# One add in four of the softmax sums is made by an accumulating DMA that GpSimd issues, in place of GpSimd's own add

## The chip, the core and the metric

One core of one Trainium2 chip. The metric is the time of one execution of the program on the device in microseconds (us), the median of several. TensorE is called PE in the profile, VectorE DVE, ScalarE ACT, GpSimd POOL and SyncE SP.

## What is computed

A small language model tower over 4096 tokens (2 sequences of 2048), width 1024, all in fp32. The attention is what the change touches: 32 heads of 32, 8 key and value heads, causal. Cut to that:

```python
h = tok_ref(x)                                # sum of 4 table rows per token, plus a bias
qkv = layernorm(h) @ w_qkv.T + b_qkv          # q: 32 heads, k and v: 8 heads, rope on q and k
scores = einsum('bhqd,bhkd->bhqk', q, k) / sqrt(HEAD_DIM)
scores = where(causal, scores, -1e20)
attn = softmax(scores, axis=-1)
out = einsum('bhqk,bhkd->bhqd', attn, v)
h = h + out @ w_o.T + b_o
h = h + ffn_ref(layernorm(h))                 # one matrix plus a low-rank Fourier update
```

## The kernel before, in words

The program has three parts. `part_a` gathers the token tables into the tile `hbuf` with indirect DMAs from GpSimd (L291): for each tile of 128 tokens one plain gather and three that add, 512 KB each, each waiting for the one before it on the same tile. In the first two chunks two tiles alternate, later four. It then makes q, k and v. `part_c` makes the output product and the last layer. Between them `part_b` does the attention, and only there does the change reach.

`part_b` goes over 16 groups of 4 heads (4 query heads share a key head). In a group, `score_steps` lists 36 steps (c, i): 256 queries c against 256 keys i, with i = c, the diagonal, first. A step has two halves of 128 keys. For each half PE makes the scores into PSUM (`st_ps`, L1097), on the diagonal VectorE adds the mask (L1012), and ScalarE takes the exponential into `probs` (L932), a ring of 8 steps in SBUF of 128 x 1024 fp32 per half. Meanwhile PE and VectorE prepare the row maxima of later rows (L1058, L984, L982), in three PSUM banks (`mx_ps`). Three steps (`LAG`) behind the scores PE multiplies `probs` with the values (L1113, `values`).

The denominators of the softmax are row sums of `probs`. To spare PE three quarters of them, GpSimd adds the tiles of `probs` first: `sum_sets` pairs the steps, and `set_sum` adds the four halves of a pair into one of four tiles `sums` of 128 x 1024 fp32, with three adds: L899 (first half plus second), L901 (plus the third), L907 (plus the fourth). PE then multiplies `sums` once with a column of ones (L1130, `denominators`), right behind the values of the pair's last step, and waits there for the sum. Of the 20 sets of a group 12 are pairs of two plain steps, 4 are pairs with a diagonal step (their last add is half as wide, 128 x 512), and 4 are a diagonal step alone (one add of 128 x 512, L895). In the last group five sets, three plain ones among them, are not summed (`unsummed`): PE takes their tiles itself (L1141).

Each engine runs its own queue in order. GpSimd's waits: for the exponential that an add reads (`exp_waited`), for its own last add (`Steps.do` waits for the semaphore that it raised), and for PE to be done with the `sums` tile that it writes again four sets later. ScalarE waits before it overwrites a slot of `probs` for the batch of values and for the sum that read it, eight steps earlier. SyncE issues the loads of the next group's queries (L89), keys (L95) and values as the present group is done with their tiles, and stores results.

Of the kernel before, what the change touches and what calls it, by code (L numbers as in the profile page):

```python
# [17 lines left out]
P = 128  # L18
# [5 lines left out]
ALU = mybir.AluOpType  # L24
# [28 lines left out]
GROUPS = ALL_HEADS // GROUP  # L53
# [497 lines left out]
STEPS, MAXES = score_steps(), max_units()  # L551
# [7 lines left out]
SLOTS, SUM_SLOTS = 8, 4  # L559
# [16 lines left out]
SETS = sum_sets()  # L576
SET_OF = [j for j, steps in enumerate(SETS) for s in steps]
# [3 lines left out]
def unsummed(g, j):  # L581

    return g == GROUPS - 1 and j in DIRECT


def sums_made(g, j):

    return g * len(SETS) + sum(not unsummed(g, k) for k in range(j + 1))


LEAD, FIRST_LEAD = 17, 14
DIAGONAL_ROOM = 0.55
TURN_AFTER = 5
# [48 lines left out]
def part_b(nc, hand, w0_hi, w0_lo, q_hi, q_lo, k_hi, k_lo, v_dram, o_dram, den_dram, recip_dram, w_o_t, w_base_t,  # L642
           w1_dram, enc, fourier_t):

    with ExitStack() as ctx:
        sb = lambda n, s, d: ctx.enter_context(nc.sbuf_tensor(n, s, d))
        sem = lambda n: ctx.enter_context(nc.semaphore(n))
# [40 lines left out]
        m_hi_done, m_rows = sem("m_hi_done"), sem("m_rows")  # L688
        st_ready, st_masked, exp_done = sem("st_ready"), sem("st_masked"), sem("exp_done")
        sum_step, sum_done, batch_done = sem("sum_step"), sem("sum_done"), sem("batch_done")  # L690
        od_copied = sem("od_copied")
        LOAD, STORE = 3 * 16, 2 * 16
        block = ctx.enter_context(nc.Block())
# [162 lines left out]
        @block.gpsimd  # L856
        def _(pool):
            nc.gpsimd.memset(k_score[M_ROW:P, :].bitcast(F32), 1.0).then_inc(k_ones_done, 1)
            pool.wait_ge(k_ones_done, 1)
            pool.wait_ge(enc_hi_done, 1)  # L860
            nc.gpsimd.tensor_tensor(enc_lo[:], enc_sb[:], enc3[0:R].bitcast(F32), ALU.subtract).then_inc(enc_lo_done, 1)
            pool.wait_ge(enc_lo_done, 1)
            pool.wait_ge(tw_hi_done, 1)
            pool.wait_ge(tw_done, 1)
            nc.gpsimd.tensor_tensor(tw_lo[:], tw[:], tw3[0:R].bitcast(F32), ALU.subtract).then_inc(tw_lo_done, 1)
            pool.wait_ge(tw_lo_done, 1)
            for c in range(DC):
                pool.wait_ge(base_in[c], 16)
                pool.wait_ge(delta_taken, c + 1)
                nc.gpsimd.tensor_tensor(hand.base[:, c, :], hand.base[:, c, :], hand.four[c][:], ALU.add  # L870
                                        ).then_inc(w1_ready, 1)

            for t in range(TPC):
                pool.wait_ge(hand.v_stored[t], 16 * CHUNKS)
            for s in range(2):
                pool.wait_ge(hand.rot_stored[s], 16 * CHUNKS * QK_TILES)
            step = Steps(pool, sum_step, 0)

            def probs_of(g, s, k, lo):
                return probs[:, (g * NS + s) % SLOTS, k, :, lo:QW]  # L880

            def exp_waited(g, s, k):
                pool.wait_ge(exp_done, 2 * (g * NS + s) + k + 1)

            def set_sum(g, j):

                q = sums_made(g, j) - 1
                at = sums[:, q % SUM_SLOTS]
                diagonal = [s for s in SETS[j] if STEPS[s][0] == STEPS[s][1]]
                wide = [(s, k) for s in SETS[j] for k in range(2) if k == 0 or s not in diagonal]  # L890
                if q >= SUM_SLOTS:
                    pool.wait_ge(batch_done, last_use[q - SUM_SLOTS] + 1)
                if len(wide) == 1:
                    exp_waited(g, diagonal[0], 1)
                    nc.gpsimd.tensor_tensor(at[:, :, P:QW], probs_of(g, diagonal[0], 0, P),  # L895
                                            probs_of(g, diagonal[0], 1, P), ALU.add).then_inc(sum_done, 1)
                    return
                exp_waited(g, *wide[1])
                step.do(nc.gpsimd.tensor_tensor(at, probs_of(g, *wide[0], 0), probs_of(g, *wide[1], 0), ALU.add))  # L899
                exp_waited(g, *wide[2])  # L900
                step.do(nc.gpsimd.tensor_tensor(at, at, probs_of(g, *wide[2], 0), ALU.add))  # L901
                if diagonal:
                    lo, last = P, (diagonal[0], 1)
                else:
                    lo, last = 0, wide[3]
                exp_waited(g, *last)
                nc.gpsimd.tensor_tensor(at[:, :, lo:QW], at[:, :, lo:QW], probs_of(g, *last, lo), ALU.add  # L907
                                        ).then_inc(sum_done, 1)

            summed = [(g, j) for g in range(GROUPS) for j in range(len(SETS)) if not unsummed(g, j)]  # L910
            last_use = [g * NS + SETS[j][-1] for g, j in summed]
            for g in range(GROUPS):
                for j in range(len(SETS)):
                    if not unsummed(g, j):
                        set_sum(g, j)

        @block.scalar
        def _(act):

            def exps(g, s, half):  # L920
                c, i = STEPS[s]
                n, lo = g * NS + s, P if i == c and half == 1 else 0
                if i == c:
                    act.wait_ge(st_masked, 2 * (g * QH + c) + half + 1)
                else:
                    act.wait_ge(st_ready, 2 * n + half + 1)
                if half == 0 and n >= SLOTS:
                    g_old, s_old = divmod(n - SLOTS, NS)
                    act.wait_ge(batch_done, n - SLOTS + 1)
                    if not unsummed(g_old, SET_OF[s_old]):  # L930
                        act.wait_ge(sum_done, sums_made(g_old, SET_OF[s_old]))
                nc.scalar.activation(probs[:, n % SLOTS, half, :, lo:QW], st_ps[:, half, :, lo:QW], ACT.Exp,  # L932
                                     scale=float(HD) ** -0.5).then_inc(exp_done, 1)

            def take(g, c):
                act.wait_ge(batch_done, g * NS + LAST_OF[c] + 1)
                if g * QH + c >= 2:
                    act.wait_ge(stored[c % 2], STORE * (g * (QH // 2) + c // 2))
                nc.scalar.copy(od_sb[:, c % 2], od_ps[:]).then_inc(od_copied, 1)  # L939

            def weight_high(c, n):
                cols = slice(n * 512, (n + 1) * 512)
                act.wait_ge(w_raw_in, 16 * (c + 1))
                nc.scalar.copy(w0_hi[:, c, cols], w_raw[:, cols]).then_inc(w0_hi_done, 1)

            def group(g, first, last):
                for s in range(NS):
                    k = s - LAG - 1
                    if k % NS in LAST_OF and not (first and k < 0):
                        take(g if k >= 0 else g - 1, LAST_OF.index(k % NS))  # L950
                    for half in range(2):
                        exps(g, s, half)
                    if 0 <= g - W_O_GROUP < DC and s in (8, 10):
                        weight_high(g - W_O_GROUP, (8, 10).index(s))

            act.wait_ge(enc_in, 16)
            nc.scalar.copy(enc3[0:R], enc_sb[:]).then_inc(enc_hi_done, 1)
            act.wait_ge(tw_ready, DC)
            nc.scalar.activation(tw3[0:R], slot_ps[0][0:R, :], ACT.Identity, scale=SCALING).then_inc(tw_hi_done, 1)
            nc.scalar.activation(tw[:], slot_ps[0][0:R, :], ACT.Identity, scale=SCALING).then_inc(tw_done, 1)  # L960
            for c in range(DC):
                act.wait_ge(delta_ready, c + 1)
                nc.scalar.copy(hand.four[c][:], slot_ps[(c + 1) % 2]).then_inc(delta_taken, 1)
            groups(group)
            take(GROUPS - 1, QH - 1)
# [78 lines left out]
        def _(pe):  # L1044
# [73 lines left out]
            def denominators(g, s):  # L1118

                c, i = STEPS[s]  # L1120
                n, j = g * NS + s, SET_OF[s]
                q = sums_made(g, j) - 1
                lo = P if SETS[j] == (s,) else 0
                pe.wait_ge(sum_done, q + 1)
                if lo:
                    for h in range(GROUP):
                        nc.tensor.matmul(od_ps[h * HD:(h + 1) * HD, 1, 0:lo], ones[:], probs[:, n % SLOTS, 0, h, 0:lo],
                                         start=False, stop=False)
                for h in range(GROUP):
                    mm = nc.tensor.matmul(od_ps[h * HD:(h + 1) * HD, 1, lo:QW], ones[:],  # L1130
                                          sums[:, q % SUM_SLOTS, h, lo:QW], start=False, stop=s in LAST_OF)
                return mm
# [412 lines left out]
```

## Time and profile before

| | us |
|---|---|
| median of 3 runs | 3373.97 (3373.56 to 3375.6) |
| the profiled execution's own time | 3371.2 |
| its span, first to last instruction | 3369.4 |
| PE busy | 3236.2 (96%) |
| GpSimd busy | 2245.7 (67%) |
| VectorE busy | 2391.3 (71%) |
| ScalarE busy | 1423.1 (42%) |
| mean granted clock of PE | 0.988 |

The profile is one execution. A row of the groups of instructions gives line, engine, operation, the tile written and those read, shapes, the number of instructions, then the busy time in us and the mean of one in ns, then the idle time just ahead of them and what ended it. A timeline row gives start and duration in us of a run of equal instructions. The attention stage runs from about 738 to 2610 us.

### The profile page before, as it was taken

How to read it: one execution, taken by the hardware profiler on the slowest of the kernel's cores; microseconds unless marked ns; L12 is line 12 of the kernel's file. 1: busy time of each engine (PE TensorE's matmuls, PEld its weight loads, DVE VectorE, ACT ScalarE, POOL GpSimd, SP SyncE). 2: the span in 40 equal slices, each digit the busy share in tenths (PEclk: the TensorE clock that was granted, in tenths of full speed). 3: DMA queues.
4: the chain of work that ended last, by engine and by line, in shares of the span. 5: the costliest groups of instructions: out<-in, count | busy, mean ns of one | idle time of the engine just before them, and what ended most of it. 6: DMA issues, size and time to landing. Idle time of an engine off the chain costs nothing. (4 is left out here: it accounts for less than half of the span.)

```text
span 3369.4 us, 59196 instructions
## 1 busy us (share of the span) xinstructions
PE 3236.2 (96%) x23824; PEld 2288.1 (68%) x23824; DVE 2391.3 (71%) x4362; ACT 1423.1 (42%) x1679; POOL 2245.7 (67%) x1033
## 2 busy tenths in 40 slices
PE   1899999999999999999999999999999899999999
PEld 1778888846666666666666666666665688888887
DVE  3667777678888888888888888888883544444443
ACT  2222222235665666666566656656656200100110
POOL 3443330049999999999999999999998222332331
PEclk8999999989999999999999999999999999999999
DMA  9999994561221222122122212212221343433342
GB/s 240 242 253 230 233 234 147 147 198 42 68 63 38 63 65 59 43 73 63 43 58 66 54 43 69 57 43 55 60 57 35 120 95 96 93 86 100 92 90 63
DMA packets 248270, 335.04 MB, mean 99 GB/s; under 512 B 64371, under 2 KB 153715, under 8 KB 247995
## 3 DMA queue, kind: packets, MB, share of 16 engines
q1 hardware_dynamic: 229562, 264.13, 29.0%
q0 software_dynamic: 18432, 67.12, 9.3%
q8 instruction: 188, 3.08, 0.4%
q14 instruction: 88, 0.71, 0.1%
HBM read 227.73 MB, written 101.71 MB: 98 GB/s over the span
## 5 line engine op out<-in xcount | busy, mean ns | idle before, releaser
L932 ACT ACTIVATE probs<-st_ps 128x1024 f32<-128x1024 f32 (+1 forms) x1152 | 1066.5, 974 | 673.4 <-PE st_ps L1097 447.2
L984 DVE TENSOR_REDUCE mpart<-mx_ps 128x1 f32<-128x512 f32 (+2 forms) x1728 | 1092.0, 683 | 196.8 <-PE mx_ps L1058 132.3
L1058 PE MATMUL mx_ps<-k_max,qs 96*128 96x512 f32 (+3 forms) x2560 | 844.2, 399 | 9.8 <-DVE mpart L984 3.2
L1097 PE MATMUL st_ps<-qs,k_score 98*128 98x512 f32 (+1 forms) x2304 | 668.3, 390 | 0.0
L1058 PEld LDWEIGHTS mx_ps<-k_max,qs 96*128 96x128 f32 x2560 | 438.8, 190 | 315.5 <-DVE mpart L984 162.3
L901 POOL TENSOR_TENSOR sums<-sums,probs 128x1024 f32<-128x1024 f32 x252 | 607.4, 2410 | 20.5 <-ACT probs L932 0.8
L899 POOL TENSOR_TENSOR sums<-probs 128x1024 f32<-128x1024 f32 x252 | 601.4, 2386 | 17.4 <-ACT probs L932 12.9
L1113 PE MATMUL od_ps<-probs,vs 128*32 128x256 f32 (+1 forms) x9216 | 589.4, 373 | 1.4 <-ACT od_sb L939 1.4
L907 POOL TENSOR_TENSOR sums<-sums,probs 128x1024 f32<-128x1024 f32 (+1 forms) x252 | 531.4, 2109 | 19.8
L1097 PEld LDWEIGHTS st_ps<-qs,k_score 98*128 98x128 f32 x2304 | 421.0, 190 | 99.2 <-ACT probs L932 24.0
L1301 POOL TENSOR_TENSOR h<-h,bb 128x1024 f32<-128x1024 f32 x32 | 104.2, 3257 | 509.5 <-DVE xn_c L1375 509.5
L1113 PEld LDWEIGHTS od_ps<-probs,vs 128*32 128x32 f32 x9216 | 240.8, 109 | 252.9 <-issue 147.4
L291 POOL DMA_INDIRECT hbuf<-in_tok_table,idx_all x128 | 194.8, 1522 | 305.9 <-DMA hbuf<-in_tok_table,idx_all 164.1
L982 DVE CUSTOM_DVE_ANT_0 mx_ps<-mx_ps,masks 128x384 f32<-128x384 f32 (+1 forms) x512 | 312.3, 645 | 53.9 <-PE mx_ps L1058 52.4
L493 PE MATMUL qk_ps<-x_hi,w_hi 128*128 128x512 f32 x640 | 253.5, 396 | 17.4 <-ACT rotation L345 15.1
L493 PE MATMUL qk_ps<-x_lo,w_hi 128*128 128x512 f32 x640 | 251.0, 392 | 0.0
L493 PE MATMUL qk_ps<-x_hi,w_lo 128*128 128x512 f32 x640 | 250.7, 392 | 0.0
L1363 DVE TENSOR_TENSOR h<-oc_ps,h_in 128x1024 f32<-128x1024 f32 x31 | 38.0, 1225 | 256.2 <-PE oc_ps L1416 256.2
L1012 DVE TENSOR_TENSOR st_ps<-st_ps,masks 128x512 f32<-128x512 f32 x256 | 168.2, 697 | 25.6 <-PE st_ps L1097 25.6
L1130 PE MATMUL od_ps<-sums,ones 128*32 128x256 f32 (+1 forms) x2520 | 180.3, 358 | 2.5 <-POOL sums L907 2.5
L1328 ACT ACTIVATE std_c<-var_c 128x1 f32<-128x1 f32 x32 | 6.5, 203 | 404.2 <-DVE var_c L1370 404.2
L1416 PE MATMUL f_ps<-w_hi,xc_hi 128*128 128x512 f32 x512 | 159.8, 394 | 6.5 <-DVE xc_lo L1385 6.5
(117 smaller groups left out, 3991.4 us busy)
## 6 DMA issues: line engine op xcount, KB each, us to landing
qs<-q_hi_scratch SPq DMA_DIRECT2D x128, 256.0 KB, 4.7
h_scratch<-hbuf SPq DMA_DIRECT2D x32, 512.0 KB, 4.4
q_hi_scratch<-rot_hi SPq DMA_DIRECT2D x64, 256.0 KB
q_lo_scratch<-rot_lo SPq DMA_DIRECT2D x64, 256.0 KB
qs<-q_lo_scratch SPq DMA_DIRECT2D x64, 256.0 KB, 5.9
o_scratch<-od_sb SPq DMA_DIRECT2D x128, 128.0 KB
o_in<-o_scratch SPq DMA_DIRECT2D x32, 512.0 KB, 4.9
o_in<-recip_scratch SPq DMA_DIRECT2D x128, 128.0 KB, 8.0
```

The source lines that it names most:

```text
L291: nc.gpsimd.indirect_dma_start(hbuf[:, m % 2, t, :], None, tables[k], bass.IndirectOffsetOnAxis(ap=idx[:, m, j:j + 1], axis=0), compute_op ...
L493: mm = nc.tensor.matmul(qk_ps[:, f % 2, :], w[a], x[b], start=(c == 0 and k == 0), stop=(c == DC - 1 and k == 2))
L899: step.do(nc.gpsimd.tensor_tensor(at, probs_of(g, *wide[0], 0), probs_of(g, *wide[1], 0), ALU.add))
L901: step.do(nc.gpsimd.tensor_tensor(at, at, probs_of(g, *wide[2], 0), ALU.add))
L907: nc.gpsimd.tensor_tensor(at[:, :, lo:QW], at[:, :, lo:QW], probs_of(g, *last, lo), ALU.add).then_inc(sum_done, 1)
L932: nc.scalar.activation(probs[:, n % SLOTS, half, :, lo:QW], st_ps[:, half, :, lo:QW], ACT.Exp, scale=float(HD) ** -0.5).then_inc(exp_done, 1)
L982: nc.vector.tensor_tensor_reduce(scored[:, 0], scored[:, 0], over, 1.0, MASKED, ALU.add, ALU.max, mpart[:, rows, kc]).then_inc(max_done, 1)
L984: nc.vector.tensor_reduce(mpart[:, rows, kc], scored, AX, ALU.max).then_inc(max_done, 1)
L1058: mm = nc.tensor.matmul(out[:, j], qs[c][0:K_ROWS, h, t * P:(t + 1) * P], k_max[0:K_ROWS, kc * CT:kc * CT + w], start=j == 0, stop=late or ...
L1097: mm = nc.tensor.matmul(out[:, :, lo:QW], k_score[0:M_ROW + 2, kt * P:(kt + 1) * P], qs[c // 2][0:M_ROW + 2, h:h + 2, at + lo:at + QW], st ...
L1113: mm = nc.tensor.matmul(od_ps[h * HD:(h + 1) * HD, 0, lo:QW], vs[:, 2 * i + k, :], probs[:, n % SLOTS, k, h, lo:QW], start=s in FIRST_OF a ...
L1130: mm = nc.tensor.matmul(od_ps[h * HD:(h + 1) * HD, 1, lo:QW], ones[:], sums[:, q % SUM_SLOTS, h, lo:QW], start=False, stop=s in LAST_OF)
```

## The change

For a set of two plain steps (`sent_along`) GpSimd no longer makes the third add. After the second add it waits for the last exponential and issues a DMA from the last half of `probs` into the `sums` tile with `accum_op=ALU.add`: the DMA engines read both and write the sum, 512 KB each. It signals one of four new semaphores `sum_sent`, one for each `sums` tile, by 16. GpSimd doesn't wait for it. PE, ahead of the denominators, and ScalarE, ahead of a slot's next use, wait for that semaphore for such sets, and for `sum_done`, with a count of its own (`sums_counted`), for the others. That makes 189 transfers: 12 in each of 16 groups less the 3 plain sets of the last group that aren't summed.

```diff
+def sent_along(g, j):
+
+    return not unsummed(g, j) and len(SETS[j]) == 2 and all(STEPS[s][0] != STEPS[s][1] for s in SETS[j])
+
+
+def sums_counted():
+
+    ended, sent, last, by_slot = {}, {}, 0, [0] * SUM_SLOTS
+    for g in range(GROUPS):
+        for j in range(len(SETS)):
+            if sent_along(g, j):
+                slot = (sums_made(g, j) - 1) % SUM_SLOTS
+                by_slot[slot] += 1
+                sent[g, j] = (slot, 16 * by_slot[slot])
+            elif not unsummed(g, j):
+                last += 1
+                ended[g, j] = last
+    return ended, sent
+
+
+ENDED, SENT = sums_counted()
...
+        sum_sent = [sem(f"sum_sent{k}") for k in range(SUM_SLOTS)]
...
                 step.do(nc.gpsimd.tensor_tensor(at, at, probs_of(g, *wide[2], 0), ALU.add))
-                if diagonal:
-                    lo, last = P, (diagonal[0], 1)
-                else:
-                    lo, last = 0, wide[3]
+                if sent_along(g, j):
+                    exp_waited(g, *wide[3])
+                    nc.gpsimd.dma_start(at, probs_of(g, *wide[3], 0), accum_op=ALU.add
+                                        ).then_inc(sum_sent[q % SUM_SLOTS], 16)
+                    return
+                lo, last = P, (diagonal[0], 1)
                 exp_waited(g, *last)
...
-                    if not unsummed(g_old, SET_OF[s_old]):
-                        act.wait_ge(sum_done, sums_made(g_old, SET_OF[s_old]))
+                    old = (g_old, SET_OF[s_old])
+                    if old in SENT:
+                        act.wait_ge(sum_sent[SENT[old][0]], SENT[old][1])
+                    elif old in ENDED:
+                        act.wait_ge(sum_done, ENDED[old])
...
-                pe.wait_ge(sum_done, q + 1)
+                if (g, j) in SENT:
+                    pe.wait_ge(sum_sent[SENT[g, j][0]], SENT[g, j][1])
+                else:
+                    pe.wait_ge(sum_done, ENDED[g, j])
```

## Rows read from the trace of the kernel before

**Rows 1.** The page: busy time (us, share, count) and slices.

```profile
PE 3236.2 (96%) x23824; PEld 2288.1 (68%) x23824; DVE 2391.3 (71%) x4362; ACT 1423.1 (42%) x1679; POOL 2245.7 (67%) x1033
...
POOL 3443330049999999999999999999998222332331
```

**Rows 2.** Stretch by stretch: length, busy of each engine, PEclk, DMA share, GB/s.

```profile
1400.00:1600.00 200.00, 199.59 (x1847) 124.87 (x1843) 173.40 (x338) 122.43 (x141) 195.77 (x90) 1.00 0.24 61
```

**Rows 3.** Groups of instructions by line, 1000 to 2400 us.

```profile
L901 POOL TENSOR_TENSOR sums<-sums,probs 128x1024 f32<-128x1024 f32 x190 | 459.6, 2419 | 14.9
L899 POOL TENSOR_TENSOR sums<-probs 128x1024 f32<-128x1024 f32 x190 | 453.4, 2386 | 3.7 <-ACT probs L932 3.4 <-issue 0.2
...
L907 POOL TENSOR_TENSOR sums<-sums,probs 128x1024 f32<-128x1024 f32 (+1 forms) x191 | 402.6, 2108 | 15.0
...
L895 POOL TENSOR_TENSOR sums<-probs 128x512 f32<-128x512 f32 x47 | 60.4, 1285 | 0.0
```

**Rows 4.** Line L907, the third add: who waited for it (us, times).

```profile
  PEld od_ps L1130: 3.4, 2
  PE od_ps L1130: 2.5, 2
```

**Rows 5.** Timeline of GpSimd in one group: start, duration (us).

```profile
1466.31 2.40 POOL L899 TENSOR_TENSOR sums<-probs 128x1024 f32<-128x1024 f32 x1
...
1474.96 2.38 POOL L901 TENSOR_TENSOR sums<-sums,probs 128x1024 f32<-128x1024 f32 x1
1477.42 2.39 POOL L907 TENSOR_TENSOR sums<-sums,probs 128x1024 f32<-128x1024 f32 x1
...
1496.37 2.39 POOL L899 TENSOR_TENSOR sums<-probs 128x1024 f32<-128x1024 f32 x1
...
1505.01 2.38 POOL L901 TENSOR_TENSOR sums<-sums,probs 128x1024 f32<-128x1024 f32 x1
...
1563.31 2.38 POOL L901 TENSOR_TENSOR sums<-sums,probs 128x1024 f32<-128x1024 f32 x1
1565.77 2.39 POOL L907 TENSOR_TENSOR sums<-sums,probs 128x1024 f32<-128x1024 f32 x1
```

**Rows 6.** Timeline of PE in the same group: the denominators of the three sets.

```profile
1483.08 0.61 PE L1130 MATMUL od_ps<-sums,ones 128*32 128x256 f32 x8
...
1511.47 0.61 PE L1130 MATMUL od_ps<-sums,ones 128*32 128x256 f32 x8
...
1568.50 0.61 PE L1130 MATMUL od_ps<-sums,ones 128*32 128x256 f32 x8
```

**Rows 7.** The gathers, line L291: durations (ns), and timeline of GpSimd.

```profile
L291 POOL DMA_INDIRECT hbuf<-in_tok_table,idx_all x128: 947/1548/3151, 3.5 to 499.6; - x128
...
26.45 1.60 POOL L291 DMA_INDIRECT hbuf<-in_tok_table,idx_all  x1 [5.45 <-DMA hbuf<-in_tok_table,idx_all]
...
35.54 1.54 POOL L291 DMA_INDIRECT hbuf<-in_tok_table,idx_all  x1 [2.90 <-DMA hbuf<-in_tok_table,idx_all]
...
50.11 1.57 POOL L291 DMA_INDIRECT hbuf<-in_tok_table,idx_all  x1 [0.30 <-issue]
55.95 1.55 POOL L291 DMA_INDIRECT hbuf<-in_tok_table,idx_all  x1 [4.27 <-DMA hbuf<-in_tok_table,idx_all]
...
62.77 1.55 POOL L291 DMA_INDIRECT hbuf<-in_tok_table,idx_all  x1 [2.74 <-DMA hbuf<-in_tok_table,idx_all]
```

**Rows 8.** DMA: the gathers' queue, and 512 KB stores by SyncE.

```profile
q0 software_dynamic: 18432, 67.12, 9.3%
...
w_scratch<-base SPq DMA_DIRECT2D x8, 512.0 KB, 2.6
```

**Rows 9.** Timeline of ScalarE: pairs of exponentials (both halves together).

```profile
1465.13 1.94 ACT L932 ACTIVATE probs<-st_ps 128x1024 f32<-128x1024 f32 x2 [0.43 <-PE st_ps L1097]
...
1494.79 1.94 ACT L932 ACTIVATE probs<-st_ps 128x1024 f32<-128x1024 f32 x2 [0.33 <-PE st_ps L1097]
```

**Rows 10.** Timeline of SyncE's queue: a query load in the same group (two of three).

```profile
1507.86 0.80 SPq L89 DMA_DIRECT2D qs<-q_hi_scratch  x2
```

## The prediction

> **What bounds the kernel now.** I read the page's busy line and slices first [rows 1]: TensorE (PE) is busy 96% of the span, GpSimd (POOL) 67%, but in the slices of the attention stage, about 740 to 2610 us, POOL stands at nine tenths as well. The busy time of a stretch inside that stage [rows 2] sharpens it: in 200 us PE works 199.6, GpSimd 195.8, VectorE 173.4, ScalarE 122.4, at a granted clock of 1.00 (2.4 GHz). So two engines have no room. The groups of instructions of 1000 to 2400 us [rows 3] say what GpSimd does: three adds of about 2.4 us for each pair of steps. It has 190 first adds in 1400 us; 16 of them belong to one group of heads, so a group takes 117.9 us, and GpSimd's adds alone (453.4 + 459.6 + 402.6 + 60.4 = 1376 of 1400 us) fill 98% of it. Yet PE hardly waits for GpSimd: 5.9 us in the whole run, four times [rows 4], all in the last group and at the start of it. PE sets the pace, with GpSimd less than 1 us a group behind it. A faster GpSimd alone therefore buys next to nothing; a later sum costs, once it comes later than PE asks for it.
>
> **How late a sum may come.** A sum is asked for by the denominators' matmuls (L1130) three steps after its last step. Three sets of the group that runs from 1444 to 1562 us show the distance, in GpSimd's order of time [rows 5] and in PE's [rows 6]. Set (8, 9): second add ends at 1474.96 + 2.38 = 1477.34, third at 1479.81, PE takes it at 1483.08. Set (17, 18): second add until 1507.39, the third by the same step until 1509.86, PE 1511.47. Set (34, 35): 1565.69, 1568.16, PE 1568.50. The last has 0.3 us to spare, the middle one 1.6, the first 3.3. From the end of the second add to the sum being ready is 2.47 us today.
>
> **Part by part.** *Removed:* 189 third adds of full width (12 sets of plain steps in each of 16 groups, less 3 that the last group leaves unsummed), 2.39 us each [rows 5], 452 us of GpSimd. The 63 half-width third adds of sets with a diagonal step stay. *Added:* 189 accumulating transfers of 512 KB, SBUF to SBUF, issued by GpSimd. The nearest rows are the accumulating gathers of the first stage, which add 512 KB of table rows into hbuf [rows 7]. Tiles 0 and 1 alternate there, so 55.95 and 62.77 are two adds into one tile, the second of which waited for the first to land. Start to start is 6.82 us, and it holds all that counts here: issue, transfer, landing, the waiting engine's waking and the launch of what follows. I take T = 6.8 us from the end of the second add to PE's release. What no row shows is a source in SBUF rather than HBM and a direct rather than an indirect transfer, which may be shorter; the fastest 512 KB transfers that SyncE issues land in 2.6 us [rows 8], so T lies between about 3.5 (2.6 and a launch) and 9.1, the same distance in a crowded stretch (26.45 to 35.54).
>
> *GpSimd's own time for it.* The issue is recorded at 1.55 us for an adding gather, 0.95 at least [rows 7]; a gap of 0.30 stands between issues that wait for nothing, and a launch after a wait is somewhat longer but not shown by itself. Estimate: 1.6 to 2.4 us for each, against 2.47 now. So GpSimd is not relieved by its 452 us but by 0.1 to 0.9 us a set, 1 to 10 us a group; its next set starts about when it did. What is queued behind the issue on GpSimd is the first add of the next set, which loses nothing.
>
> *On the path.* The sum is ready 6.8 - 2.5 = 4.3 us later than today, if GpSimd starts as now. It can't start much earlier at the places that matter, since there it waits for ScalarE. Set (8, 9) follows (6, 7), whose first add waits for the first exponential of step 7, over at 1465.13 + 0.97 = 1466.1 [rows 9]; it starts at 1466.31, so 0.2 us may be won. PE: 1477.34 - 0.2 + 6.8 = 1483.9 against 1483.08, a wait of 0.9. Set (17, 18) follows (15, 16), whose first add starts at 1496.37 and may start at 1494.79 + 0.97 = 1495.8, 0.55 earlier: 1507.39 - 0.55 + 6.8 = 1513.6 against 1511.47, a wait of 2.2. Set (34, 35): 1565.69 + 6.8 = 1572.5 against 1568.50, but PE is 3.1 us later by now and GpSimd has won part of that: 0.9 remain, up to 1.4 if GpSimd wins nothing, 0.5 if it wins most. Two neighbours, (19, 20) and (32, 33), have spare times like these and bring 0.3 to 0.8 between them. The other seven sets come out with time to spare, above all once PE's lateness of 3 us counts, since it gives every later sum so much more time. Together 4.6 us a group (3.9 to 5.3), 69 us in 15 groups. In the last group no row maxima follow, the steps get shorter, and two sums are already waited for [rows 4]; there 4.3 us later means about 9 us over several sets. Sum: 78.
>
> *Collisions.* The loads of the next group's queries, 3 of 256 KB, are issued from 1507.86 on [rows 10], just when set (17, 18)'s transfer would run, and again at the group's end beside set (34, 35). They use the same 16 DMA engines. The queue of the gathers took 9.3% of the engines' span for 67 MB [rows 8], that is 313 us of all 16 engines for 128 transfers, 2.4 us each; so the 189 new ones add some 460 us of it to a stage whose engines are a fifth to a quarter busy [rows 2]. I put 0.5 us on two sets a group, 15 us in all. Against it stands what PE catches up: after a stop VectorE has emptied its row maxima, and PE meets fewer full banks for a while; I put 13 us. Edits at nothing: ScalarE's wait for a slot's old sum lies four steps (some 13 us) behind the landing, and the four new semaphores only replace one. Result 3371.2 + 80 = 3451 in terms of the profiled execution, whose span is 3369.4; the median of the runs is 2.8 us above it, so 3454.
>
> **A page against the row.** The fixed part and rate that a page gives would bring the sum in time. The Trainium skill (DMA: Bandwidth & Descriptors, Anatomy of one DMA — SWDGE (gpsimd) path) gives about 2.0 us plus bytes over 436 GB/s for a DMA of this path, 3.2 us for 512 KB by my estimate from it; by that the first rival below would hold. The trace speaks against it for accumulating ones: 6.82 us per dependent step in [rows 7].
>
> **Rivals.** (a) *The transfer is in time, no slower than before.* It decides at T = 4.6 us: set (17, 18) has 1511.47 - 1506.84. Source and target in SBUF and a transfer of 2.6 us as in [rows 8] would give about 3.5, and then no set waits; PE even loses up to 5.9 us of waits [rows 4]. Time 3368 to 3376. Against it: every adding gather took longer. (b) *The transfer is as slow as in the crowded stretch*, T = 9.1, because both ends lie in SBUF or the loads get in between. Then seven or eight sets a group wait, by the same walk 14 us a group: 3371 + 225, 3600. For it: the collision with the query loads; against it: the DMA engines are mostly free. (c) *GpSimd becomes the bound.* The longest issue of a gather took 3.15 us [rows 7]. With a launch that makes 4 us in place of 2.47, 12 x 1.5 us = 18 us a group, less the 1 us that it had to spare, so some +270: 3645. For it: 98% busy; against it: the median issue is 1.55. (d) *A short issue and T near 5.5*, direct and from SBUF: only (17, 18) and a bit of (8, 9) wait, 1 to 1.5 us a group, +20 to +25: 3396.
>
> **Chances.** Forecast with its own range 3420 to 3500: 0.50. (a) 0.09, (b) 0.14, (c) 0.07, (d) 0.20. The range leaves out (a) and (c) and half of the far end of (b): 3385 to 3570. A measurement of this kernel can tell about 0.2%, 7 us, from no change. Faster by more needs (a) and a gain beyond the 5.9 us: 0.03. Within 0.2%: 0.07. Slower: 0.90.
>
> **What would show it.** GpSimd's busy share in the attention stage stays at eight to nine tenths or falls little (the issues recorded at 1.0 to 1.6 us each, 189 of them); PE waits for the DMA into sums at L1130, 4 to 6 us a group, mostly at sets (8, 9) and (17, 18) and at the group's end; the groups lie 122 to 123 us apart in place of 117.8; VectorE and ScalarE durations are unchanged. I am wrong in T if the wait is at every set or at none; wrong in GpSimd's price if its share rises to ten tenths, or if the issue is so short that it idles by a third; and wrong in the walk if PE's waits add up to one amount and the groups stretch by another.

## The result, and the profile after

The changed kernel takes 3503.4 us (median of 4 runs, 3491.2 to 3512.2) against 3373.8 beside it: 1.0381 times as long, with an interval of 1.0343 to 1.0418. The forecast was 3454 with a range of 3385 to 3570, slower. The profiled execution took 3510.1 us, 3508.3 of it the span, 138.9 more than before.

The added lines shift the line numbers: in the changed kernel GpSimd's first and second add are L921 and L923, the issue of the transfer is L926, and the denominators are L1160.

The page of the changed kernel: busy line, slices of GpSimd, the queue of GpSimd's transfers, the groups of its first add, issue and the denominators, and the landing time of the new transfers.

```profile
PE 3300.4 (94%) x23824; PEld 2316.2 (66%) x23824; DVE 2409.6 (69%) x4362; ACT 1424.7 (41%) x1679; POOL 1954.6 (56%) x1033
...
POOL 3443220167777777777777777787776322333221
...
q0 software_dynamic: 45648, 166.22, 24.0%
...
L921 POOL TENSOR_TENSOR sums<-probs 128x1024 f32<-128x1024 f32 x252 | 609.8, 2420 | 329.3 <-ACT probs L959 318.4
...
L1160 PE MATMUL od_ps<-sums,ones 128*32 128x256 f32 (+1 forms) x2520 | 187.4, 370 | 73.0 <-DMA sums<-probs 72.9
...
L926 POOL DMA_DIRECT2D sums<-probs x189 | 161.9, 857 | 59.7 <-POOL sums L923 49.4
...
sums<-probs POOLq DMA_DIRECT2D x189, 512.0 KB, 4.8
```

Three readings against [rows 1]. GpSimd fell from 67 to 56% and from nine tenths to seven or eight in the attention stage; it hardly waited for its first add before [rows 3], and now stands idle ahead of it for 318 us until ScalarE's exponentials come. So GpSimd is relieved. TensorE waits 72.9 us at the denominators for the new transfers. And TensorE is *busy* 3300.4 us with the same 23824 matmuls that took 3236.2: 64.2 us more. Idle time grew from 133.2 to 207.9 us (span less busy), by 74.7. The two add up to the 138.9 of the span. Half of the loss is waiting, and the other half is slower work, which the forecast did not have.

Where the slower work lies is seen in the windows (length, busy of each engine, PEclk, DMA share, GB/s; a packet counts whole in the window in which it starts, so a short window can show a DMA share above 1). One is like that of [rows 2], one lies behind a stop in the middle of a group of heads, and three lie around the stop at the group's end.

```profile
1400.00:1600.00 200.00, 191.03 (x1701) 118.53 (x1697) 161.94 (x323) 112.84 (x128) 151.16 (x82) 0.97 0.46 99
1440.50:1442.00 1.50, 1.50 (x5) 1.21 (x4) 1.29 (x2) 0.03 (x1) 0.85 (x1) 0.50 1.10 212
1494.50:1501.00 6.50, 3.68 (x36) 1.78 (x28) 4.02 (x12) 3.37 (x4) 3.77 (x3) 1.00 0.82 176
1501.90:1508.70 6.80, 6.80 (x47) 4.70 (x44) 3.72 (x6) 2.68 (x4) 2.85 (x3) 0.50 0.78 187
1508.70:1515.00 6.30, 6.30 (x57) 3.62 (x56) 5.57 (x11) 3.94 (x5) 3.91 (x2) 0.99 0.19 64
```

In the third row TensorE works 3.68 of 6.5 us; in the fourth it is granted 0.50, the lower of its two levels (1.2 GHz), for 6.8 us; then full clock again. The second row is such a stretch too, behind a shorter stop. One such stretch, of 10.2 us, stands at the first exponentials in every run. Behind it the stage had none before, and has 22 after, 122.9 us together, which costs about half of that, 61 us: nearly all the 64.2 of the busy line.

The two stops, engine by engine (start, duration, idle time before it and its releaser). GpSimd's queue:

```profile
1430.50 2.38 POOL L923 TENSOR_TENSOR sums<-sums,probs 128x1024 f32<-128x1024 f32 x1
1433.18 0.86 POOL L926 DMA_DIRECT2D sums<-probs  x1 [0.30 <-POOL sums L923]
...
1488.47 2.38 POOL L923 TENSOR_TENSOR sums<-sums,probs 128x1024 f32<-128x1024 f32 x1 [0.35 <-ACT probs L959]
1491.15 0.85 POOL L926 DMA_DIRECT2D sums<-probs  x1 [0.30 <-POOL sums L923]
```

TensorE:

```profile
1439.58 0.64 PE L1160 MATMUL od_ps<-sums,ones 128*32 128x256 f32 x8 [2.01 <-DMA sums<-probs]
...
1495.58 1.14 PE L1124 MATMUL st_ps<-qs,k_score 98*128 98x512 f32 x4
...
1501.42 0.64 PE L1160 MATMUL od_ps<-sums,ones 128*32 128x256 f32 x8 [3.24 <-DMA sums<-probs]
...
1502.59 1.48 PE L1124 MATMUL st_ps<-qs,k_score 98*128 98x512 f32 x4
```

The four score matmuls behind the second stop take 1.48 us. The same four, in the same place behind the sum of (34, 35), took 0.86 in the kernel before:

```profile
1569.39 0.86 PE L1097 MATMUL st_ps<-qs,k_score 98*128 98x512 f32 x4
```

SyncE's query loads in the same stretch:

```profile
1433.77 0.80 SPq L89 DMA_DIRECT2D qs<-q_hi_scratch  x2
...
1490.20 0.98 SPq L89 DMA_DIRECT2D qs<-q_hi_scratch  x2
```

Set (17, 18): second add over at 1432.88, TensorE released at 1439.58, 6.7 us. Set (34, 35): 1490.85 to 1501.42, 10.6 us. Both have a query load beside them. Over the stretch of 1415 to 1510 us the tile view of sums gives the time from an issue to its waiter's release:

```profile
DMA to landing us min/median/max: 4.5/5.1/10.2
```

The smallest, 4.5, is the transfer left alone (its last packet ends 4.2 us after the issue, and the signal follows 0.3 later); with the 0.30 us of launch it makes T = 4.8. A third thing is seen beside it: the issue costs GpSimd 0.30 + 0.86 = 1.16 us where the add took 2.47.

### The profile page after: what moved, and what is told of

Read it like the earlier page. It is cut to its first block and busy times, and to the rows that moved or that the text cites. A ratio compares the mean times of both kernels' runs of the same rounds, so it can differ in the third digit from the quotient of the medians.

```text
span 3508.3 us, 59196 instructions
## 1 busy us (share of the span) xinstructions
PE 3300.4 (94%) x23824; PEld 2316.2 (66%) x23824; DVE 2409.6 (69%) x4362; ACT 1424.7 (41%) x1679; POOL 1954.6 (56%) x1033
## 5 line engine op out<-in xcount | busy, mean ns | idle before, releaser
L1085 PE MATMUL mx_ps<-k_max,qs 96*128 96x512 f32 (+3 forms) x2560 | 862.7, 407 | 12.9 <-DVE mpart L1011 6.0
L921 POOL TENSOR_TENSOR sums<-probs 128x1024 f32<-128x1024 f32 x252 | 609.8, 2420 | 329.3 <-ACT probs L959 318.4
L1124 PE MATMUL st_ps<-qs,k_score 98*128 98x512 f32 (+1 forms) x2304 | 684.9, 399 | 2.4 <-ACT probs L959 2.4
L1085 PEld LDWEIGHTS mx_ps<-k_max,qs 96*128 96x128 f32 x2560 | 449.1, 194 | 322.9 <-DVE mpart L1011 158.6
L923 POOL TENSOR_TENSOR sums<-sums,probs 128x1024 f32<-128x1024 f32 x252 | 599.3, 2378 | 49.5 <-ACT probs L959 34.5
L1140 PE MATMUL od_ps<-probs,vs 128*32 128x256 f32 (+1 forms) x9216 | 602.4, 380 | 2.0 <-ACT od_sb L966 2.0
L1124 PEld LDWEIGHTS st_ps<-qs,k_score 98*128 98x128 f32 x2304 | 433.4, 196 | 107.8 <-ACT probs L959 28.3
L291 POOL DMA_INDIRECT hbuf<-in_tok_table,idx_all x128 | 192.9, 1507 | 306.5 <-DMA hbuf<-in_tok_table,idx_all 167.2
L1160 PE MATMUL od_ps<-sums,ones 128*32 128x256 f32 (+1 forms) x2520 | 187.4, 370 | 73.0 <-DMA sums<-probs 72.9
L926 POOL DMA_DIRECT2D sums<-probs x189 | 161.9, 857 | 59.7 <-POOL sums L923 49.4
```

Source lines behind the costliest of these rows:

```text
L291: nc.gpsimd.indirect_dma_start(hbuf[:, m % 2, t, :], None, tables[k], bass.IndirectOffsetOnAxis(ap=idx[:, m, j:j + 1], axis=0), compute_op ...
L1085: mm = nc.tensor.matmul(out[:, j], qs[c][0:K_ROWS, h, t * P:(t + 1) * P], k_max[0:K_ROWS, kc * CT:kc * CT + w], start=j == 0, stop=late or ...
L1124: mm = nc.tensor.matmul(out[:, :, lo:QW], k_score[0:M_ROW + 2, kt * P:(kt + 1) * P], qs[c // 2][0:M_ROW + 2, h:h + 2, at + lo:at + QW], st ...
L1140: mm = nc.tensor.matmul(od_ps[h * HD:(h + 1) * HD, 0, lo:QW], vs[:, 2 * i + k, :], probs[:, n % SLOTS, k, h, lo:QW], start=s in FIRST_OF a ...
```

## The experiments

All comparisons are ratios to the kernel before on the same chip. The distance of groups is that from one group's first exponential to the next one's, 117.8 us before; groups are counted from 0.

**TensorE doesn't wait for the landing.**

```diff
-                if (g, j) in SENT:
-                    pe.wait_ge(sum_sent[...], SENT[g, j][1])
-                else:
+                if (g, j) not in SENT:
                     pe.wait_ge(sum_done, ENDED[g, j])
...
+                                          probs[:, n % SLOTS, 0, h, :] if (g, j) in SENT else
```

> The changed kernel, but PE's denominators of the 189 sent sets read a tile of exponentials that has long been there and don't wait for the transfer (part of the sums is left out of the result; the transfers, GpSimd's adds and issues, and ScalarE's wait for a slot all stay). Theory A, the sums come late and PE's clock falls after the stops: both gone, 3365 to 3380 us, granted clock back at 0.987. Rival B, the 99 MB of transfers and the issues slow the stage by themselves: 3480 to 3500, as the changed kernel.

In TensorE's place GpSimd now waits for a landing, but only before it writes the same tile of `sums` again, four sets later; ScalarE's wait is as it was. Measured 3385.8 us against 3370.0, ratio 1.0054 (1.0036 to 1.0072). The 189 transfers still run. TensorE never stops at a denominator, nothing falls to half clock behind the first exponentials, and with that 3.3 of the 3.8% are gone. The DMA traffic and GpSimd's issues by themselves cost little; the waits are what counts. But 16 us remain where at most 10 were expected: groups 2 to 9 are 119.0 us apart (one of them 119.9), where most others keep their 117.8. That was a new question. A small part is the traffic: three times TensorE waits for a query load, 3.1 us together, which it never did before.

**The three latest sets are added by GpSimd again, nine are sent.**

```diff
-    return not unsummed(g, j) and len(SETS[j]) == 2 and ...
+    return j not in (5, 10, 19) and not unsummed(g, j) and len(SETS[j]) == 2 and ...
...
-                lo, last = P, (diagonal[0], 1)
+                lo, last = (P, (diagonal[0], 1)) if diagonal else (0, wide[3])
```

> The changed kernel, with the own third add of before in sets (8, 9), (17, 18) and (34, 35) of each group; the other nine are sent. Theory A (only these three are late): 3368 to 3382, no wait for a transfer at the denominators. Rival B (traffic): three quarters of the loss stay, about 3470.

Measured 3401.2, ratio 1.0086 (1.0069 to 1.0103): three sets in twelve, (8, 9), (17, 18) and (34, 35), carry three quarters of the loss. It is more than expected. The neighbour (19, 20), which had been covered by the stop at (17, 18), is now late itself by some 0.7 us in each group. The larger part lies in groups 2 to 9: in the profiled execution, the slowest of the four, they are 31.7 us longer together than before. In six of them a subtraction on VectorE takes 2.9 us (0.68 before) and TensorE stops behind it, here in group 2:

```profile
1016.20 2.92 DVE L1044 TENSOR_TENSOR w_lo<-w_raw,w_hi 128x512 fp32r<-128x512 f32 x1
```

```profile
1019.78 0.50 PE L1085 MATMUL mx_ps<-k_max,qs 96*128 96x512 f32 x1 [1.48 <-DVE mpart L1011]
```

Five of these six stops were followed by 3.4 us at half clock. What makes the subtraction long comes out further down.

**Only the last set, (34, 35), is sent.** The same edit with `j == 19`.

> The kernel before, with only set (34, 35) of each of 15 groups sent, 15 transfers. Theory A: it collides with the query load at the group's end, PE waits 2 to 4 us each time and its clock falls for some microseconds, 4.5 to 6 us a group: 3440 to 3465. Rival B: 15 of 189 transfers, 10 us: 3384.

Measured 3441.6, ratio 1.0215 (1.0193 to 1.0236), the time as expected. The waits of TensorE in this kernel, first row (us in total, times, longest):

```profile
PE od_ps L1160 <- DMA sums<-probs: 38.5, 15, 3.9
```

38.5 us of waits lengthen the span by 70. TensorE's busy time is 3270.6, 34.4 more than before: 68.3 us at half clock in 13 stretches. So one transfer a group costs over half of the whole change, about half of it by the wait and half by the clock. But the collision that was expected is mostly missing. One of the 15, with the query load, the issue and the stop:

```profile
857.11 0.98 SPq L89 DMA_DIRECT2D qs<-q_hi_scratch  x2
```

```profile
861.96 0.93 POOL L926 DMA_DIRECT2D sums<-probs  x1 [0.31 <-POOL sums L923]
```

```profile
867.00 1.00 PE L1160 MATMUL od_ps<-sums,ones 128*32 128x256 f32 x8 [1.92 <-DMA sums<-probs]
```

Here GpSimd still makes all its other adds, so the issue comes some 5 us behind the load and not 0.9, and the transfer lands 5.4 us behind its issue (median) against 8.9 in the changed kernel. TensorE stops all the same, 2.6 us on the mean, since without GpSimd's relief it asks for the sum some 3.2 us after the second add (2.8 in the kernel before [rows 5, 6]), and even the 4.8 of a transfer left alone is too long for that.

**The query loads beside the transfers are left out.**

```diff
-                            load_q(g + 1, c)
+                            if c < 2:
+                                load_q(g + 1, c)
```

> The changed kernel without the loads of the next group's queries 1024 to 2047 (c = 2 and 3; the first group's stay in their place, so part of the computation is left out). Theory A with the collision as its cause: transfers of sets (17, 18) and (34, 35) land 4.5 to 4.8 us after the second add as the others do, waits shrink to under 0.5 us a group: 3372 to 3390. Rival C, these sets are late for another reason (GpSimd's order of work): waits and time stay within 20 us of 3500.

Measured 3402.0, ratio 1.0102 (1.0082 to 1.0121), above the 3372 to 3390 expected. What it was made for came out: without these loads set (17, 18) lands 4.5 us after its issue and (34, 35) 4.6 (medians), in place of 6.4 and 8.9, and the waits of TensorE are

```profile
PE od_ps L1161 <- DMA sums<-probs: 14.4, 17, 5.9
```

against 72.9. The collision with the query loads is thus 2.8 of the 3.8%, some 94 us; in the profiled executions the difference is 108.5 us, 58.5 of it waits and about 53 the clock behind them. What is left over the expectation lies in groups 2 to 9 (119.4 us apart in place of 118.0) and in the last group, 12.9 us longer than before. One stop of 2.7 us there is at T = 4.9. The longest stop of the run is there too, and its transfer, issued just behind other loads of SyncE for the last part, lands only after 11.5 us (12.0 in the changed kernel, whose longest stop, 5.5 us, is the same one):

```profile
2562.33 0.34 SPq L800 DMA_DIRECT2D w_in<-w_scratch  x1
```

```profile
2562.63 0.85 POOL L927 DMA_DIRECT2D sums<-probs  x1 [0.30 <-POOL sums L924]
```

```profile
2574.18 1.08 PE L1161 MATMUL od_ps<-sums,ones 128*32 128x256 f32 x8 [5.92 <-DMA sums<-probs]
```

**A late sum without a transfer.** In (34, 35) GpSimd makes its own third add after three needless ones; the sets (8, 9), (17, 18) and (19, 20) are added by GpSimd as before, the other eight are sent. The run without the needless adds is the next one.

```diff
+                for _ in range(3 if j == 19 else 0):
+                    step.do(nc.gpsimd.tensor_tensor(at, at, probs_of(g, *last, 0), ALU.add))
```

> As the next kernel (eight sets sent), but in set (34, 35), which GpSimd adds itself, three more adds of full width stand ahead of the last (the sum is then another): its sum comes some 7.4 us later, with no transfer and no query load in its way. By the slack of the next kernel, 4.7 us, PE waits about 2.7 us once in each of 15 groups; GpSimd has room for the adds. Theory A, the clock falls after such a stop whatever causes it: half-speed stretches of 3 to 7 us behind each, 5 to 6 us a group, 3440 to 3460. Rival, the lower clock came with the transfers: the waits alone, 3405 to 3415 at a granted clock of 0.987.

Measured 3454.8, ratio 1.0242 (1.0226 to 1.0257), inside what was expected if the clock follows the stop and not the DMA. TensorE's waits, then one stop, then the windows before and after it:

```profile
PE od_ps L1162 <- POOL sums L933: 40.3, 17, 2.5
```

```profile
1485.18 0.77 PE L1162 MATMUL od_ps<-sums,ones 128*32 128x256 f32 x8 [2.51 <-POOL sums L933]
...
1486.46 1.49 PE L1126 MATMUL st_ps<-qs,k_score 98*128 98x512 f32 x4
```

```profile
1482.00:1485.10 3.10, 0.67 (x15) 0.13 (x4) 1.09 (x5) 0.70 (x1) 3.02 (x3) 1.00 0.02 1
1485.70:1489.00 3.30, 3.30 (x18) 2.12 (x18) 2.13 (x4) 1.29 (x2) 3.22 (x3) 0.50 0.51 142
```

The DMA engines were idle in the stop (0.02), GpSimd was adding, and the clock fell all the same: 58.0 us at half clock in 12 stretches. So it is the stop that brings the lower clock and not the transfer; the stops of 1.5 us that VectorE caused in the nine-sent kernel say the same. Not every stop does: 11 of the 15 in (34, 35) were followed by such a stretch (the twelfth lies in the last group, behind a wait for ScalarE of 3.0 us), and none of the eight stops of 1.0 us in the eight-sent kernel below was.

**Eight are sent,** (8, 9), (17, 18), (19, 20) and (34, 35) are not.

```diff
+    return j not in (5, 10, 11, 19) and ...
```

> The changed kernel, with GpSimd's own third add in sets (8, 9), (17, 18), (19, 20) and (34, 35); eight of twelve are sent. Theory A: no wait for a sum in groups 1 to 14, so nothing lost but what VectorE's weight subtraction loses beside GpSimd (some 1 us in each of eight groups), and nothing gained either, since PE sets the pace: 3366 to 3382. If a relieved GpSimd were worth something, it would be below 3363.

Measured 3389.2, ratio 1.0044 (1.0031 to 1.0058), 7 us above the expectation. Groups without weight work are exactly 117.8 us apart, though GpSimd has much less to do in them: its relief is worth nothing. The rest, 15 us, is two things: groups 2 to 9 (119.0 each, 10 us together) and the last group, 5.0 us longer. TensorE's waits show the first, eight stops of one us:

```profile
PE st_ps L1124 <- ACT probs L959: 8.2, 8, 1.1
```

Each lies behind a subtraction on VectorE, w_lo<-w_raw,w_hi, of which two stand in each of groups 2 to 9. The line takes part in the change nowhere, but its duration moved. Before, VectorE and GpSimd:

```profile
1254.85 1.28 DVE L1017 TENSOR_TENSOR w_lo<-w_raw,w_hi 128x512 fp32r<-128x512 f32 x1
```

```profile
1253.21 2.38 POOL L899 TENSOR_TENSOR sums<-probs 128x1024 f32<-128x1024 f32 x1
```

The same subtraction, the second of group 4, in the changed kernel:

```profile
1286.50 1.79 DVE L1044 TENSOR_TENSOR w_lo<-w_raw,w_hi 128x512 fp32r<-128x512 f32 x1
```

```profile
1285.37 2.38 POOL L923 TENSOR_TENSOR sums<-sums,probs 128x1024 f32<-128x1024 f32 x1 [0.65 <-ACT probs L959]
```

In both the subtraction begins inside an add and ends some 0.55 us after it: 1256.13 against 1255.59, and 1288.29 against 1287.75. Its length is what was left of the add, plus 0.55. The first subtraction of a group took 0.68 us before and meets an add too in the changed kernel, 1.87 us in group 4. With eight sets sent the second one of each group meets an add nearly whole and takes 2.53 us.

**More sums in the last group.** Eight sent, and in the last group only the last two sets stay unsummed, to give TensorE fewer denominators.

```diff
-DIRECT = [len(SETS) - k for k in (8, 6, 4, 2, 1)]
+DIRECT = [len(SETS) - k for k in (2, 1)]
```

> As the kernel before this one, and in the last group only the last two sets stay unsummed rather than five, since GpSimd now has room: PE saves some 24 matmuls of 0.056 us for each of two plain sets and half of that for the third. Gain of 2 to 4 us against the kernel before this one if the sums come in time; the same or slower if they don't.

Measured 3393.2, ratio 1.0057 (1.0043 to 1.0071): no gain, the second branch of the expectation. The last group is 6.3 us longer than with eight sent alone, since added sums are asked for before they are there (three stops of 3.4, 0.7 and 2.7 us).

**The subtraction is moved.** Eight sent; the second weight subtraction is put behind step 15, where GpSimd idles in every group.

```diff
-                    if 0 <= g - W_O_GROUP < DC and s in (12, 14):
-                        weight_low(g - W_O_GROUP, (12, 14).index(s))
+                    if 0 <= g - W_O_GROUP < DC and s in (12, 15):
+                        weight_low(g - W_O_GROUP, (12, 15).index(s))
```

> Eight of the twelve sets are sent, as in the run before; the only edit is that the second of the two weight subtractions on VectorE (L1044 of the changed kernel's line numbers) is put behind step 15 instead of step 14, where GpSimd has been idle for some 3 us in each group. Theory: the subtraction and GpSimd's adds shut each other out, and with eight sets sent the second one begins inside an add (2.5 us instead of 0.7), which is the 1.2 us by which groups 2 to 9 are longer. It should fall back to 0.7 to 1.2 us, TensorE's stop of 1.0 us beside it should go, groups 2 to 9 should come down from 119.0 to 117.8 us, and the time from 3389 to 3378 to 3382 us. Rival: the groups with weights are longer for another reason (the weights' own loads beside the landings): they stay at 119.0 us and the time at 3387 to 3392 us. Second rival: the new place delays VectorE's maxima behind step 15; the groups then get longer than 119.0 us, time over 3395 us.

Measured 3385.7 against 3379.5 beside it, ratio 1.0014 (1.0003 to 1.0025), 0.3% or 10 us less than the eight-sent kernel; in terms of the kernel before at 3374.9, where that one ran, 3379.6. The moved subtraction takes 0.68 us in all eight groups, and five of these are 117.9 us apart. The other three are 119.7, 121.2 and 121.2, and in just these three the *first* subtraction, not moved, took 2.91 us in place of 0.68. VectorE, in a long group and in a short one:

```profile
1014.76 2.91 DVE L1044 TENSOR_TENSOR w_lo<-w_raw,w_hi 128x512 fp32r<-128x512 f32 x1
```

```profile
1134.43 0.68 DVE L1044 TENSOR_TENSOR w_lo<-w_raw,w_hi 128x512 fp32r<-128x512 f32 x1
```

GpSimd in the same two:

```profile
1014.74 2.38 POOL L923 TENSOR_TENSOR sums<-sums,probs 128x1024 f32<-128x1024 f32 x1
```

```profile
1134.46 2.90 POOL L923 TENSOR_TENSOR sums<-sums,probs 128x1024 f32<-128x1024 f32 x1
```

Both times the two begin within 0.03 us of each other, right behind GpSimd's first add. Where GpSimd began first (1014.74), its add keeps its 2.38 us and VectorE ends 0.55 us behind it; where VectorE began first (1134.43), it keeps its 0.68 us and the add takes 0.52 longer. These two instructions don't share, the later one is shut out. That agrees with the Trainium skill (SBUF — State Buffer, SBUF: two separate sides), by which a VectorE instruction with two SBUF inputs contends with a GpSimd instruction that reads SBUF, and whoever starts first has the shared port pair for its whole instruction.

The three long groups differ though the subtraction is equally long in them. Behind it TensorE stops for 1.49 us, waiting for VectorE's maxima, in all three. In the two groups of 121.2 us 3.4 us at half clock followed, in the one of 119.7 none did. The stop and the window behind it in one of the two:

```profile
1609.73 0.50 PE L1085 MATMUL mx_ps<-k_max,qs 96*128 96x512 f32 x1 [1.49 <-DVE mpart L1011]
```

```profile
1610.50:1613.90 3.40, 3.40 (x36) 2.52 (x29) 1.85 (x4) 0.00 (x0) 1.58 (x1) 0.50 0.71 135
```

**And the last group's adds are GpSimd's own.** `g < GROUPS - 1` is added to the condition.

> As the run with the moved subtraction, and in the last group GpSimd makes every add itself. Theory: the last group is the only one with fewer waits for ScalarE, so the landings there are late (2 us each at two sets); with its own adds it takes 103.5 us again instead of 108.6, and the time is that of the kernel before within 0.2% (3370 to 3378 us), although GpSimd is relieved of seven or eight adds in each of fifteen groups. Rival: taking adds from GpSimd gives something back once nothing is late any more: under 3365 us. Second rival: something of the sending stays that no stop shows: over 3382 us.

Measured 3382.6 against 3379.5, ratio 1.0007 (0.9996 to 1.0017): no difference from the kernel before, as the theory had it (3377 in terms of 3374.9). The last group is 105.8 us to its last exponential, 3.8 less than in the run above it and 2.3 more than before. GpSimd is busy 2062 us against 2246, so 184 us of its work are gone and nothing is gained. The first subtraction still takes 2.91 us in three groups, which are 7 us longer together; no run moves that one. But the plain groups, which it doesn't touch, are 117.8 us apart as before. No version tried here beats the kernel before.

## Why the prediction came out, and where it did not

The time lies in the range and the sign is right, but it is 49 us above the forecast and just outside the narrower 3420 to 3500 that had a chance of 0.50. Two terms of the sum were wrong and hid each other, and a third was not in it. The prediction's last sign of being wrong, that the waits add up to one amount and the groups stretch by another, is what happened: 4.3 us of stops a group, and groups 126.3 us apart on the mean, 8.5 more than before, where 122 to 123 were forecast.

**TensorE sets the pace; a faster GpSimd buys nothing; only lateness costs.** Right. The eight-sent kernel's plain groups take exactly 117.8 us, and without the waits for the landing 3.3 of the 3.8% are gone. One reading under it was off: the 5.9 us and four times of [rows 4] count a matmul and its weight load twice. TensorE stopped twice, 2.5 us together, at 2571.5 and 2578.7, in the second half of the last group and not at its start. So rival (a) had at most 2.5 us to win.

**T = 6.8 us.** Mis-sized for a transfer left alone: 4.8. The gathers' 6.82 of [rows 7] was the shortest of four such distances on its two tiles (which are 2 and 3, not 0 and 1; the others are 7.1 to 8.4), so a reading of the gathers' mean would have been further off. It holds an issue of 1.55 us against 0.86 here; how the rest divides between the table in HBM and the indirect addresses no run separates. Rival (d) had foreseen the direction, and 4.8 lies close to rival (a)'s point of decision, 4.6. The Trainium skill's figure (DMA: Bandwidth & Descriptors, Anatomy of one DMA — SWDGE (gpsimd) path), 3.2 us by my estimate from it, is short of the 4.5 us from issue to landing that the runs show for this accumulating one.

**Collisions, 0.5 us on two sets a group.** Mis-sized the other way, and the larger fault. The sets and the cause were named rightly, the query loads of [rows 10], but the transfers landed 1.8 us later at (17, 18) and 4.2 us later at (34, 35). Leaving these loads out took 58.5 us of waits, where the sum had 15, and with the clock behind them 2.8% of the time, about 94 us. The forecast took the mean busy share of the DMA engines, a fifth to a quarter [rows 2]. What counts is what is in them when the transfer is issued. At (34, 35) its first packet starts some 4.2 us after the issue (median) in place of 1.4, and in that time, here behind the issue at 1491.15, the engines were busy for others:

```profile
1490.60:1495.50 4.90, 4.90 (x53) 2.75 (x52) 4.90 (x13) 2.70 (x4) 2.37 (x3) 1.00 0.82 135
```

All packets in this window are of SyncE's queue.

**The walk.** By sets, in us a group, stops measured over 14 groups:

| set | forecast | measured | why |
| --- | --- | --- | --- |
| (8, 9) | 0.9 | 0.2 | T about 5.5, between 5.0 and 6.7 |
| (17, 18) | 2.2 | 2.2 | T of 6.7 (median): 4.8 and 1.9 by the query loads, together the 6.8 of the forecast |
| (34, 35) | 0.9 | 1.9 | T of 9.3 on the mean, but GpSimd further ahead |
| neighbours | 0.3 to 0.8 | 0 | only late once (17, 18) is not |

The sum of the stops was 78 us in the forecast and is 73 here. That is a near hit by luck: too long a T and too small a collision cancel in it.

**GpSimd's price of an issue, 1.6 to 2.4 us.** Mis-sized: 1.16. The step that followed from it, that GpSimd is hardly relieved and its next set starts about when it did, fails; its slices fell to seven or eight tenths. At (34, 35) that changed two things. TensorE was ready at 1498.18, 7.3 us after the second add, where it was 2.8 before [rows 5, 6] and 3.2 in the run that sends only this set, so there were some 4 us more to spare. But the issue moved forward too, from 5 us behind the query load to 0.9, and the mean T of this set grew from 5.8 to 9.3. Little is left of the lead: stops of 1.9 in place of 2.6 us. Without the query loads the same lead is enough, and TensorE never waits for this set. Elsewhere the relief bought nothing.

**Catch-up of 13 us.** Not seen: idle time and slower work already fill the span's growth of 138.9.

**What was missing.** TensorE's clock, some 61 us, is the whole of the distance between forecast and result and more. The stops of 2 to 3 us were forecast, but priced at their own length. And VectorE's subtraction, about 10 us where nothing else covers it: a step priced at nothing, because its line is not touched, though its partner on the shared path had moved by a few tenths of a us. In the changed kernel itself its share can't be parted from the stops. That VectorE's durations stay unchanged, as forecast, fails with it.

Rival (b), T = 9.1 because the loads get in between, was true of one set in twelve; (c) never came near; (a) failed at the collisions. Without them it was nearly true of the plain groups, 118.0 us in place of 117.8, and not of the kernel, which was still 1.0% slower. No run moves the query loads elsewhere and keeps them; whether a kernel that sends the sums can then come level stays open.

## What to carry to other kernels

A stop of TensorE of 2 to 3 us in otherwise full work cost 1.6 to 1.9 times its length in these runs: look for the clock in the windows behind it. For a transfer put on a path with little to spare, look up which loads are issued in the very microseconds around it, not the mean load of the DMA engines, and look at the place where it will stand after the change: an engine that is relieved issues earlier, and here that moved the transfer into the loads. And before an engine is relieved, ask who waits for it: here TensorE did for 2.5 us in the whole run, so 184 us less work was worth nothing, while sums that TensorE wants less than T after the second add each made it stop.

## What the runs showed of the hardware that I had not expected

- In the changed kernel most stops of 1.8 to 3.4 us (20 of 24, by the records of the granted clock) were followed by 3.4 or 6.8 us at 0.50, and 11 of 15 stops of 2.5 us that no transfer caused were too. Of twelve stops of 1.5 us behind VectorE, in the nine-sent kernel and the last two, eight were. Of the eight stops of 1.0 us in the eight-sent kernel none was.
- A direct accumulating transfer of 512 KB within SBUF lands 4.5 us after its issue when alone, 6.4 when a query load of three times 256 KB is issued 0.6 us behind it, and 8.9 (median, 10.2 at most) when that load is issued 0.9 us before it.
- Its issue holds GpSimd for 0.86 us, after a launch of 0.30.
- A VectorE subtraction of two SBUF operands takes 0.68 us or 2.91, by whether it begins 0.03 us before or 0.02 us after a GpSimd add.
